# A seq-to-seq model's first attention, written out unit by unit, with its result divided and split in transposed layout

## What is computed

```python
x = x + attention0(layernorm(x))        # 16 heads of width 16, causal, with q, k, v and o projections
x = x + experts(layernorm(x))           # router, top 2 of 8 experts (F = 512), and one shared gated MLP
x = x + attention1(layernorm(x))        # one head of width 256, causal
x = x + mlp(layernorm(x))               # ternary weights, 256 -> 1024 -> 256, relu
```

```python
scores = jnp.einsum('bhqd,bhkd->bhqk', q, k) / sqrt(d_k) + mask
attn = jax.nn.softmax(scores, axis=-1)
out = jnp.einsum('bhqk,bhkd->bhqd', attn, v)
out = out.transpose(0, 2, 1, 3).reshape(b, s, -1)
return jnp.einsum('bsv,mv->bsm', out, o_proj_weight)
```

## Time and profile before

| | us |
|---|---|
| whole kernel, median of three runs (lowest, highest) | 1905.46 (1896.89, 1908.47) |
| the profiled execution, its time | 1900.88 |
| its span, first to last instruction | 1898.7 |
| projections: 3.65 to last load landed, about | 129 |
| first attention, first instruction to the next phase's | 134.46 to 720.57 |
| token stage (output projection, router, shared MLP) | 720.57 to about 955 |
| experts, second attention, MLP | to 1898.7 |

### The profile page before, as it was taken

The page is one execution under the profiler, slowest core; times in us unless marked ns, Lnnn a source line. Parts: engine busy times, 40 slices in busy tenths (PEclk is TensorE's granted clock), DMA queues, the critical chain, the costliest instruction groups (busy, mean ns, idle before and its releaser), DMA issues. The chain is left out here.

```text
span 1898.7 us, 32866 instructions
## 1 busy us (share of the span) xinstructions
PE 1638.8 (86%) x10403; PEld 1123.0 (59%) x10404; DVE 766.5 (40%) x1692; ACT 972.0 (51%) x1548; POOL 463.5 (24%) x496
## 2 busy tenths in 40 slices
PE   5928998998998995999819999999848987898898
PEld 4812322322322324888718888888637986797787
DVE  6720100101101004777653333333265556665785
ACT  3727998997997993444332222222223434333342
POOL 3013111101111111445651222222213104000664
PEclk9968998998998997999959999999978997898999
DMA  5675336236246006411141111111132000000001
GB/s 172 222 145 74 40 44 78 36 48 78 34 50 78 10 7 195 156 47 45 49 137 45 50 52 50 53 50 50 42 100 67 23 26 31 1 1 4 19 27 45
DMA packets 96348, 117.77 MB, mean 62 GB/s; under 512 B 40608, under 2 KB 75040, under 8 KB 93088
## 3 DMA queue, kind: packets, MB, share of 16 engines
q1 hardware_dynamic: 89696, 98.25, 23.7%
q0 software_dynamic: 6528, 17.87, 2.6%
HBM read 70.43 MB, written 45.65 MB: 61 GB/s over the span
## 5 line engine op out<-in xcount | busy, mean ns | idle before, releaser
L668 ACT ACTIVATE probs<-ps_s 128x1024 f32<-128x1024 f32 (+3 forms) x640 | 512.1, 971 | 55.6 <-PE ps_s L718 54.6
L732 PE MATMUL ps_o<-probs,V_unit 128*17 128x512 f32 (+3 forms) x2560 | 305.2, 544 | 9.9 <-POOL probs L653 7.8
L653 POOL TENSOR_SCALAR_AFFINE_SELECT probs<-probs 128x512 f32<-128x512 f32 x128 | 81.5, 637 | 484.3 <-ACT probs L668 482.4
L685 DVE COPY weighted<-ps_o 128x512 f32<-128x512 f32 x32 | 22.1, 692 | 405.3 <-PE ps_o L732 405.3
L718 PE MATMUL ps_s<-Q_even,K_even 64*128 64x512 f32 (+3 forms) x640 | 130.9, 465 | 52.5 <-DVE V_unit L679 33.8
L718 PEld LDWEIGHTS ps_s<-Q_even,K_even 64*128 64x128 f32 x640 | 59.0, 198 | 185.8 <-ACT probs L668 132.8
L1424 PE MATMUL ps_slot_y<-we_out,slot_hT 128*128 x576 | 136.3, 380 | 0.9 <-DVE slot_hT L1371 0.9
L718 PEld LDWEIGHTS ps_s<-Q_odd,K_odd 64*128 64x128 f32 x640 | 55.1, 183 | 135.0 <-ACT probs L668 126.8
L1894 POOL TENSOR_TENSOR h_lo<-h,h_hi 128x512 fp32r<-128x512 f32 x64 | 89.4, 1414 | 183.8 <-DVE h L1940 183.8
L718 PE MATMUL ps_s<-Q_odd,K_odd 64*128 64x512 f32 (+3 forms) x640 | 125.3, 442 | 7.7 <-ACT probs L668 6.3
L1371 DVE COPY slot_hT<-ps_hT 128x512 f32<-128x512 f32 x72 | 49.8, 692 | 195.5 <-PE ps_hT L1414 192.6
(11 more groups left out here) (274 smaller groups left out, 3855.6 us busy)
## 6 DMA issues: line engine op xcount, KB each, us to landing
slot_rows<-slots_in SPq DMA_DIRECT2D x72, 128.5 KB
qk_parts<-qk_hi SPq DMA_DIRECT2D x8, 1024.0 KB, 4.3
qk_parts<-qk_lo SPq DMA_DIRECT2D x8, 1024.0 KB, 6.9
Q_even<-qk_parts SPq DMA_DIRECT2D x24, 256.0 KB
K_even<-qk_parts SPq DMA_DIRECT2D x24, 256.0 KB
Q_odd<-qk_parts SPq DMA_DIRECT2D x24, 256.0 KB
K_odd<-qk_parts SPq DMA_DIRECT2D x24, 256.0 KB
X<-x SPq DMA_DIRECT2D x8, 512.0 KB, 4.7
```

What stands on the lines that cost most here:

```text
L653: pool.affine_select(out=block_of, in_=block_of, compare_op=ALU.is_ge, fill=0.0, base=0, pattern=[[0, HG], [1, P]], channel_multiplier=-1) ...
L668: act.activation(probs[:, g % PROB_BUFS, 2 * p:2 * p + 2, off:BT], ps_s[:, s % SCORE_BUFS, :, off:BT], ACT.Exp).then_inc(exp_ok, 1)
L732: last = pe.matmul(ps_o[32 * h:32 * h + DH + 1, q % 2, off:BT], V[:, j, t, h, :], probs[:, g % PROB_BUFS, h, off:BT], start=(t == 0), stop ...
```

## The change

- **Weights at the head.** Each of wq, wk, wv has its own semaphore. ScalarE rounds wq alone, splits block 0, then rounds wk and wv; VectorE makes w_lo in three parts.
- **POOL at the head.** The four memsets of `blank_rows` wait for the third w_lo. After them POOL, no longer SP, issues the first unit's twelve loads, when the stores of blocks 0 to 3 have landed, and waits for them.
- **Order.** The attention is straight code: 320 steps that overlap all the way, no loop. A unit is now (group u % 4, batch u // 4), so batch 0 comes first. TensorE reads V in place; `V_unit` and its copies go.
- **Slice end.** VectorE copies the half, rounds it and takes the difference. Two products with a 0/1 matrix (`pick`, made by POOL) spread each head's denominator over its 32 rows, over the same half of `ps_o`. VectorE takes the reciprocal of 128x512, multiplies, rounds and takes the difference, in transposed layout. The first product into a half waits for the reciprocal of two slices ago. SP stores eight pieces of 16 x 512 a slice, four heads of hi and of lo, to `attended_parts`.
- **Token stage.** `load` brings `aT_hi` and `aT_lo` (two buffers each) by two DMAs, 1 MB a block where it was 0.5 MB. `turn_a` and its splits go; step i is project(i), turn_x(i-1), contract(i-2), scores(i-1), expand(i-1), count_rows(i-1).

The core of the diff:

```diff
             def _(sp):
...
-                    if b == SEQ // BT + 2:
-
-                        for parity in range(2):
-                            sp.wait_ge(parts_out[parity], 32 * (SEQ // BT // 2))
-                        sp.wait_ge(blank_ok, 4)
-                        load_stacks(sp, io, 0, 0, k["first_stacks"][0], k["first_stacks"][1], k["loaded"][0])
...
             def _(pool):
                 pool.memset(zeros[:, :], 0.0).then_inc(zero_ok, 1)
                 pool.wait_ge(zero_ok, 1)
+                pool.wait_ge(w_lo_ok, 3)
                 blank_rows(pool, k["first_stacks"][0], k["first_stacks"][1], 1.0, blank_ok)
+                for parity in range(2):
+                    pool.wait_ge(parts_out[parity], 32 * (SEQ // BT // 2))
+                load_stacks(pool, io, 0, 0, k["first_stacks"][0], k["first_stacks"][1], k["first_in"])
+                pool.wait_ge(k["first_in"], 16 * STACK_LOADS)
...
-                act.wait_ge(w_in, 48)
-                act.activation(w_hi[:, :], w_raw[:, :], ACT.Copy).then_inc(w_split, 1)
+                act.wait_ge(w_in[0], 16)
+                act.activation(w_hi[:, 0], w_raw[:, 0], ACT.Copy).then_inc(w_hi_ok, 1)
                 highs(0, 0)
+                for n in (1, 2):
+                    act.wait_ge(w_in[n], 16)
+                    act.activation(w_hi[:, n], w_raw[:, n], ACT.Copy).then_inc(w_hi_ok, 1)
...
+                        dve.wait_ge(pv_ok, NT * u + LAST[q] + 1)
                         dve.tensor_copy(sums[:, q % 2], ps_o[:, q % 2]).then_inc(sums_ok, 1)
+                        dve.wait_ge(sums_ok, 3 * n + 1)
+                        dve.tensor_copy(sums_hi[:, :], sums[:, q % 2]).then_inc(sums_ok, 1)
+                        dve.wait_ge(sums_ok, 3 * n + 2)
+                        dve.tensor_tensor(sums_lo[:, :], sums[:, q % 2], sums_hi[:, :].bitcast(F32), ALU.subtract
+                                          ).then_inc(sums_ok, 1)
+                        dve.wait_ge(picked_ok, n + 1)
+                        dve.reciprocal(inv[:, :], ps_o[:, q % 2]).then_inc(norm_ok, 1)
+                        dve.wait_ge(norm_ok, 3 * n + 1)
+                        dve.tensor_tensor(result[:, :], sums[:, q % 2], inv[:, :], ALU.mult).then_inc(norm_ok, 1)
+                        dve.wait_ge(norm_ok, 3 * n + 2)
+                        if n >= 2:
+                            dve.wait_ge(stored[q % 2], 16 * ROWS_OUT * (n // 2))
+                        dve.tensor_copy(out_hi[:, q % 2], result[:, :]).then_inc(norm_ok, 1)
+                        dve.wait_ge(norm_ok, 3 * n + 3)
+                        dve.tensor_tensor(out_lo[:, q % 2], result[:, :], out_hi[:, q % 2].bitcast(F32), ALU.subtract
+                                          ).then_inc(result_ok, 1)
...
+                    if t == 0 and n >= 2:
+                        pe.wait_ge(norm_ok, 3 * (n - 2) + 1)
...
+                    pe.wait_ge(sums_ok, 3 * n + 3)
+                    rows = pick[:, :, :].rearrange("p h r -> p (h r)")
+                    pe.matmul(ps_o[:, q % 2], rows, sums_hi[:, :], start=True, stop=False)
+                    pe.matmul(ps_o[:, q % 2], rows, sums_lo[:, :], start=False, stop=True).then_inc(picked_ok, 1)
...
-                    if live(i + 1):
-                        turn_a(i + 1, 1 - j, n + j)
```

More of the change, by code:

```diff
@@ L376, in _ @@
                 lows(0, 0)
+                for n in (1, 2):
+                    low_weights(n)
                 over_blocks(dve, BLOCKS, body)
@@ L417, in body @@
                         w, o = c // DC, (c % DC) * P
+                        if is_first(i) and c % 2 == 0:
+                            pe.wait_ge(w_lo_ok, w + 1)
                         for d in range(DC):
@@ L581, in phase_attention @@
     DIAG = [g for g, (q, t, _) in enumerate(TILE_LIST) if t >= TB * q]
+    STEPS = [(u, g) for u in range(UNITS) for g in range(NT)]
     SCORE_BUFS, PROB_BUFS = 3, 4
@@ L644, in _ @@
                 blank_rows(pool, Q[1], K[1], 1.0, blank_ok)
-                with pool.Fori(0, UNITS // 2) as n:
-                    for j in range(2):
-                        u = 2 * n + j
-                        for g in DIAG:
-                            off = TILE_LIST[g][2]
-                            block_of = probs[:, g % PROB_BUFS, :, off:off + P]
-                            hold(pool, k, exp_ok, 2 * NT * u + 2 * g + 2 + 2)
-                            pool.affine_select(out=block_of, in_=block_of, compare_op=ALU.is_ge, fill=0.0, base=0,
-                                               pattern=[[0, HG], [1, P]], channel_multiplier=-1).then_inc(mask_ok, 1)
+                pool.memset(pick_f32[:, :, :], 0.0).then_inc(pick_ok, 1)
@@ L695, in _ @@
-                take_v(0, 0)
-                take_v(1, 1)
-                with dve.Fori(0, UNITS // 2 - 1) as n:
-                    for j in range(2):
-                        unit(2 * n + j, j, n)
-                        take_v(2 * n + j + 2, j)
-                for j in range(2):
-                    unit(UNITS - 2 + j, j, UNITS // 2 - 1)
+                        dve.wait_ge(sums_ok, 3 * n + 1)
+                        dve.tensor_copy(sums_hi[:, :], sums[:, q % 2]).then_inc(sums_ok, 1)
+                        dve.wait_ge(sums_ok, 3 * n + 2)
@@ L707, in _, with scores @@
                 pe.wait_ge(zero_ok, 1)
-                def scores(u, j, g):
+                def scores(at):
+                    u, g = STEPS[at]
+                    j = u % 2
                     q, t, off = TILE_LIST[g]
+                    if g == 0:
+                        pe.wait_ge(loaded[j], 16 * LOADS * (u // 2 + 1))
                     for p in range(2):
-                        s = 2 * g + p
-                        before = s - SCORE_BUFS if s >= SCORE_BUFS else max(
-                            x for x in range(2 * NT) if x % SCORE_BUFS == s % SCORE_BUFS) - 2 * NT
-                        pe.wait_ge(exp_ok, 2 * NT * u + before + 1 + 2)
+                        s = 2 * at + p
+                        if s >= SCORE_BUFS:
+                            pe.wait_ge(exp_ok, s - SCORE_BUFS + 1)
@@ L873, in load @@
                     b, t0 = i * BT // SEQ, i * BT % SEQ
-                    for g in range(GROUPS):
-                        sp.dma_start(rows[:, i % 2, :, g, :],
-                                     io["attended"][g, b, t0:t0 + BT, :].rearrange("(t p) c -> p t c", p=P)
+                    for n, part in enumerate((aT_hi, aT_lo)):
+                        sp.dma_start(part[:, i % 2].bitcast(F32),
+                                     io["attended"][n, b].rearrange("(c p) t -> p c t", p=P)[:, :, t0:t0 + BT]
                                      ).then_inc(rows_in[i % 2], 16)
@@ L2014, in program @@
         k = {"nc": nc, "io": io}
-        k["passed"], k["residual_ok"] = (ctx.enter_context(nc.semaphore(name)) for name in ("passed", "residual_ok"))
+        k["passed"], k["residual_ok"], k["first_in"] = (
+            ctx.enter_context(nc.semaphore(name)) for name in ("passed", "residual_ok", "first_unit_in"))
         k["X"] = ctx.enter_context(nc.sbuf_tensor("X", [P, TILES, D], F32))
```

216 lines of the change are left out of this document (98 added, 118 removed).

## The result

| us | before | after |
|---|---|---|
| median of five runs each (lowest, highest) | 1904.88 (1896.89, 1908.47) | 1891.64 (1886.14, 1894.29) |
| the profiled execution, its time | 1900.88 | 1889.35 |
| first attention begins | 134.46 | 135.29 |
| first attention lasts | 586.1 | 576.6 |
| token stage, first load to last product of `count_rows` | 221.6 | 220.7 |

The ratio is 0.994, 95% interval 0.9921 to 0.9959: 13 us less by the medians, where I had forecast 23 less, inside the range. The interval lies clear of 1, so the kernel is 0.6% faster, but it is no change at the 1% that I had set. Three stages missed, and the misses partly cancelled: attention gave more than twice what I said, the projections and the token stage almost nothing of their 16 us.

A forecast was written before the change was run, and what follows sets the result against it. In the first attention ScalarE was taken as the bound (511.7 us busy of 566), with other losses at single places. Loads -4, attention -4 and token stage -12 make -20: 1900.9 becomes 1881, as a median 1882, range 1866 to 1896.

The forecast's parts named there:

- the loads' sum: End of projections: loads and stores of blocks 4 to 7 end at 125 against 129 if DMA never idles, -4 us.
- token stage: Token stage: earlier start and six further turnings off TensorE, together -12 us, bounds -5.5 and -20.
- nearly all path, since TensorE is 90% busy: Token stage steps: six further turnings of 1.03 us leave TensorE and nearly all count, -6.2 us.
- start of attention (head and loads): Before the first attention: gain 0 at the head, -4 us from the twelve loads moved to POOL.
- loop turns: First attention: straight code has no loop turns, three times (75.5 - 67.4) us saved, -24 us.
- reciprocal's wait: Attention, slice 0 after slice 3: TensorE waits 1.2 to 1.5 us a unit, seven units, +10.5 us.
- tail: End of attention: last copy to next stage takes 14.3 us instead of 4.7, +9.6 us.
- Head: Head: projections start 8 us earlier, but memsets then block block 1's xn until 31.9; gain 0, cold restart costs 3.
- C: End of projections: block 4's stores share with the loads, block 6 waits up to 16 us; 1885 to 1887, chance 0.12.
- rival A: Attention's slice end and tail: the 512-column reciprocal takes only 0.69 us; total 1868 us, chance 0.12.
- The 5.5 us: Token stage start: first projection about 3.5 us earlier and two waits behind aT_lo gone, together -5.5 us.
- rival D: Token stage: TensorE's saved turnings don't count because another wait fills their place; total 1887 us, chance 0.13.

The follow-up runs named there:

- e4: Changed kernel with a plain copy in place of VectorE's 512-column reciprocal, leaving the division out: 1880.18 us, attention 569.2 us.
- e1: Changed kernel with the head of the kernel before (weights waited for together, fills not waiting), loads still on POOL: 1882.75 us, attention from 132.69.
- e3: Changed kernel with the first unit's twelve loads back on SP behind block 5's stores: attention begins at 136.59 us.
- e10: Changed kernel with the twelve loads on SP, three ahead of the stores of each of blocks 4 to 7: attention begins at 124.86 us.
- e12: Changed kernel with eight unused transposes of xn per block where the removed turning stood: middle token steps 25.2, 25.1, 25.6, 25.0, 25.2 us.
- e11: Kernel before with GpSimd's first h_lo after four scatters instead of six: middle token steps 25.25, 25.40, 25.62, 25.05, 24.90 us.
- e5: Changed kernel with each token block's eight xn transposes issued twice, ahead of GpSimd's chain: middle steps 25.87, 27.34, 25.54, 25.74, 25.75 us.
- e9: Changed kernel with GpSimd's first h_lo after four scatters instead of six: middle token steps 24.4, 24.1, 24.8, 24.2, 24.2 us.
- e13: Changed kernel with POOL's fills spaced by the blocks' xn, e10, e9 and three smaller reorderings: 1860.44 us, ratio 0.9797 to the kernel before.

## Why the prediction was wrong in part

I forecast 23 us less and 13 came. Two steps failed, each for its own reason: the loads' sum ("if the DMA engines never idle"), and the token stage ("nearly all path, since TensorE is 90% busy"). The wait for the reciprocal was mis-sized the other way, 3.3 us instead of 10.5, and that attention's surplus of 5.5 us hid a third of the 16 us that the two lacked is luck.

| term | forecast | measured, from |
|---|---|---|
| start of attention (head and loads) | -4 | +1.6, means of three profiles before and six after |
| loop turns | -24 | -23.3, e4's pitches against the first profile |
| reciprocal's wait | +10.5 | +3.3 (e4), 2.8 by the row of waits |
| tail | +9.6 | +8.6 to 9.0 |
| attention in all | -4 | -9.5; -12.2 as means of three and nine |
| token stage | -12 | -0.9 profiled; -1.7 as means of two and seven; -5.5 in e1 and e4, where no step drops to 0.94 |
| sum | -20 | -11.5 profiled, -13.2 by medians |

**Head: right.** xn blocked from 20.6 to 31.7 and the cold restart came as written (forecast 31.9). I said 3 us later behind it; it is 1.2 to 2.4 by block 0's stores.

**The twelve loads: wrong in the step "if the DMA engines never idle".** The sentence carried its own exception, "unless block 6 has to wait for block 4's buffers", and I gave that case 0.12. It happened in every profile with the loads on GpSimd: 17.3 to 18.7 us of ScalarE's wait, a little over my "up to 16". Of C's two prices for block 4's stores the one from rows (104 instead of 83, 21 us more) came true, the lower one (9 to 15 more) did not. While ScalarE waits, nothing new reaches the queue, and when the loads are done the engines run dry between the last stores. The end stays where it was, e3 shows the other arrangement with the same end, and e10 shows that the sum's condition needed an order in which neither happens; the sum then asked for 6 us too much.

**Loop turns: right**, to within 1 us against the first profile (-25 against the second). Every pitch is now 67.95 without the reciprocal's part, so the pitches behind a turn shrank by 0.6 to 0.9 and the first one grew by 0.7; I had left both in.

**Reciprocal: duration nearly right, wait three times too large.** 3.36 us for 512 columns, where the slope gave 3.9 and my estimate from the repeat count in the Trainium skill (VectorE: DVE Perf Modes, "Walkthrough: the 8-slice pipeline in each mode") 4.4; rival A (0.69) is out. The mis-sized term is the 1.2 to 1.5 us a unit, which measured 0.40 by the waits and 0.47 by e4. After the reciprocal's start VectorE needs 7.1 us until the next sums are ready (223.66 to 230.7), where I had 7.75 to 8.05, and TensorE is ready 6.7 us after it, not 6.6. A difference of two long times close to each other carries all the error of both; and the 0.4 for GpSimd's masks, which I added on top, does not appear on this path.

**Tail: right** within 1 us (13.27 to 13.65 in the two profiles, forecast 14.3).

**Token stage: wrong twice.** *Start.* The 5.5 us did appear: x is first turned 20.9 us into the stage instead of 26.2. But the first projection, which I had 3.5 us earlier, gained 0.6 (9.2 us into the stage, 9.8 before): the weights' split waits for the router's load, which now stands behind the larger loads of the first block, and begins at 7.7 instead of 5.9. And I wrote "the shared weights' split on VectorE limits" and still counted the whole. ScalarE's rounding of the shared weights begins 14.7 us into the stage (13.1 before; presumably because the attention parts ahead of them are twice the bytes, which no run isolated), and xn waits for a square root queued behind it; the low parts of the turned x (`xn2T_lo`) stand behind VectorE's three differences of the weights; and TensorE, which waited 4.46 and 3.83 us, runs the first expansion at a clock of 0.72 averaged over that step, against 0.93 and 0.85 in the two profiles before. Measured at the first `ps_mid` the gain is 2 to 3 us (30.4 on average of seven against 31.9 and 33.7), at the second turning of xn some 2. *Steps.* "Nearly all path, since TensorE is 90% busy" is the step that failed, and rival D (0.13) named it. A busy share says how much room there is for a wait, not whether the removed work was in the chain that closes a step. It was in for 0.4 of 1.03 (e12, e11), and then a third of the middle steps took 1.6 us more at a granted clock of 0.94.

The traces show where that clock fell. In each of the 12 slow steps, and in e5's one, there is one stretch of 3.4 us at the lower of the two levels (0.50, which is 1.2 GHz; 1.00 is 2.4), and it begins within 1.6 us behind the end of TensorE's pause for the second h_shared. In step 2 of the changed kernel:

```profile
777.76 0.50 PE L116 MATMUL ps_gated<-xn2T_hi,w_swiglu_hi 128*128 128x512 f32 x1 [2.03 <-DVE h_shared L1135]
```
```profile
778.80:782.20 3.40, 3.40 (x9) 2.63 (x8) 0.69 (x1) 0.69 (x2) 2.74 (x3) 0.50 0.11 39
```

Before these 13 falls the pause had lasted 1.89 to 2.03 us. In the seven profiles with the token stage as changed, steps 2, 3 and 5 have such a pause (1.89 to 2.03) and 12 of those 21 were slow; step 4 has one of 1.34 and step 6 one of 1.46 to 1.75, and none of those 14 was. Where no pause of a middle step was longer than 1.56 us (three profiles of the kernel before, e9, e12 and e13, 30 steps) none was slow either. With the turning taken out the pause is longer: in steps 2 and 3 it is 1.35 and 1.56 us in the second profile of the kernel before, 2.02 and 1.92 in that of the changed kernel.

What stays open: why only some of the steps with the longer pause were slow, and why e1 and e4 had none in the same code. No run altered the pause alone, so that the pause brings the lower clock is argued from these counts, not shown.

## What to carry to other kernels

Work taken from the busiest engine pays only if it stands in the chain that closes the step, so follow that chain in one step's timelines, across the engines that look idle (here GpSimd's six scatters), before multiplying a saving by the number of steps. When a big transfer moves to another queue, ask which buffer the next producer needs back and lay the pieces between the stores: order alone gave 11 us here, the other queue 2 at most. And an operation that blocks another engine should not be moved "later" but into a stretch where that engine runs nothing that it can block.

## What the hardware showed that I had not expected

- Loads of 256 KB into 16 partitions run at 121 GB/s alone and hold all DMA engines while they do; stores alone run at 398. Beside the loads on the other queue, the 2 MB of block 4's stores took 29 us (issued from 75.96, buffer free at 105.05) against 8 alone, and both together moved 168 to 176 GB/s. Neither queue went first.
- VectorE's reciprocal took 3.36 us for 512 columns, 258 ns for 16 and 171 ns for 4: 6.3 ns a column, without the start.
- The same code differed by 9.7 us in the unchanged rest between profiles (951.9 to 961.6), and by 3 us at the start of attention. Single profiles can't weigh a change of a few microseconds in their totals; the changed kernel's pitches in attention can: 60 of 63 in nine profiles lie within 0.03 us of each other.
